# Four-head layer: one matmul for a bound per head, the bias added on GpSimd, normalization and stores inside the loop

## The reference, cut to what matters

```python
x = layernorm(y)                                  # input of the layer, per node over 128 features
Q, K, V = (einsum('bnd,hde->bhne', x, W) for W in (Wq, Wk, Wv))
scores = einsum('bhne,bhme->bhnm', Q, K) / sqrt(32)
scores = where(adj > 0, scores, -inf)
heads = einsum('bhnm,bhme->bhne', softmax(scores, -1), V)
out = concat(heads) @ Wo.T + bo                   # bo: 128 values
y = out + x
result = layernorm(y)
```

## Time and profile before

| | us |
|---|---|
| median of three runs | 1037.8 |
| profiled execution, device time | 1042.1 |
| its span | 1038.0 |
| four-head layer, first to last nb | 674.6 to 981.0 |
| last normalization phase, first operation | 996.1 |
| final check, first operation | 1032.9 |

### The profile page before, as it was taken

How to read it: one execution, slowest core, us unless ns; L and a number is a source line. 1 busy time by engine, 2 the same in 40 slices (tenths; PEclk the granted TensorE clock), 3 DMA queues, 4 the chain that set the end, 5 groups by cost and what they waited for, 6 DMA issues and landing times. The chain is left out here.

```text
span 1038.0 us, 27673 instructions
## 1 busy us (share of the span) xinstructions
PE 783.3 (75%) x9034; PEld 546.0 (53%) x9066; DVE 723.8 (70%) x1912; ACT 508.3 (49%) x1102; POOL 394.5 (38%) x615
## 2 busy tenths in 40 slices
PE   2888888888883777773767776599999999999800
PEld 1555655565652566662555554356665666666500
DVE  2278878888884788895688877455656656556487
ACT  0444444444443888872565666255444554444410
POOL 1455555555641244432555555222222222223100
PEclk9989989999997999996999999699999999999955
DMA  4123333332311122220122222101101011011034
GB/s 118 37 52 77 76 76 76 76 76 76 76 33 21 22 32 30 31 30 11 21 30 26 25 25 25 16 11 17 16 10 15 10 15 15 10 15 16 2 139 185
DMA packets 34627, 43.42 MB, mean 42 GB/s; under 512 B 4361, under 2 KB 22290, under 8 KB 34578
## 3 DMA queue, kind: packets, MB, share of 16 engines
q0 software_dynamic: 18576, 16.82, 12.6%
q1 hardware_dynamic: 16002, 25.97, 8.0%
HBM read 51.19 MB, written 8.39 MB: 57 GB/s over the span
## 5 line engine op out<-in xcount | busy, mean ns | idle before, releaser
L405 DVE SCALAR_TENSOR_TENSOR pp<-banks,floor,adj 128x1024 f32<-128x1024 f32 x128 | 162.1, 1270 | 1.2 <-PE banks L496 1.2
L1081 ACT ACTIVATE pp<-banks,nb 128x512 f32<-128x512 f32 x128 | 81.4, 695 | 85.1 <-issue 59.6
L1049 POOL TENSOR_TENSOR q<-qt 128x512 bf16<-128x512 f32 x32 | 33.0, 1030 | 234.0 <-ACT qt L1074 234.0
L603 DVE TENSOR_SCALAR x<-yres,mean,rstd 128x128 f32 (+1 forms) x256 | 96.6, 439 | 1.8 <-PEq L1752 1.5
L496 PE MATMUL banks<-rows 32*128 32x128 bf16 x1024 | 59.1, 223 | 40.0 <-DVE pp L405 37.4
L509 PE MATMUL banks<-pp,yv 128*17 128x128 f32 x2048 | 84.7, 285 | 1.4 <-DVE pp L405 1.3
L343 ACT COPY rows<-banks 128x640 bf16<-128x640 bf16 x64 | 44.3, 692 | 65.3 <-PE banks L486 65.2
L975 PE MATMUL banks<-w,xt 128*128 128x256 f32 x256 | 73.3, 386 | 0.0
L640 POOL TENSOR_TENSOR yres<-oo,x 128x512 f32 (+1 forms) x32 | 40.3, 1259 | 85.2 <-DVE oo L745 85.2
L348 ACT COPY ot<-banks 128x512 f32<-128x512 f32 x64 | 37.5, 585 | 67.0 <-PE banks L509 66.9
L275 POOL TENSOR_TENSOR yv<-wh,yv 128x512 f32<-128x512 f32 x32 | 35.2, 1099 | 88.3 <-ACT yv L336 88.3
(11 more groups left out here) (198 smaller groups left out, 2151.9 us busy)
## 6 DMA issues: line engine op xcount, KB each, us to landing
adj<-in_adjt POOLq DMA_DIRECT2D x96, 128.0 KB, 3.0
xt<-in_xt SPq DMA_DIRECT2D x32, 256.0 KB, 3.6
x<-in_x SPq DMA_DIRECT2D x32, 256.0 KB, 3.0
out_ngd<-xo SPq DMA_DIRECT2D x32, 256.0 KB, 2.0
adj<-in_adj POOLq DMA_DIRECT2D x32, 128.0 KB, 3.0
ident<-in_ident SPq DMA_DIRECT2D x1, 64.0 KB, 1.9
w<-in_w SPq DMA_DIRECT2D x1, 64.0 KB, 1.8
w0t<-in_w0t SPq DMA_DIRECT2D x1, 64.0 KB, 2.2
```

Source lines behind the costliest of these rows:

```text
L405: nc.vector.scalar_tensor_tensor(pp[:, g], S[g % 2][:, :].rearrange("p (h n) -> p h n", n=N), floor[:, slot:slot + 1], adj[:, slot, g:g + ...
L603: ins = nc.vector.tensor_scalar(xr[:, slot, g, :], yres[:, bass.ds(at, 1), :].rearrange("p o d -> p (o d)"), mean[:, bass.ds(at, 1)], rstd ...
L1081: nc.scalar.activation(pp[:, slot % 2, h], S[h][:, :], ACT.Exp, bias=nb[:, slot % 2:slot % 2 + 1], scale=SCALE).then_inc(s["p"], 1)
```

## The change

It does these things in heads and around it:
- One value bounded the scores of all heads. Now there is one per head: fm, the column maximum, is broadcast as the stationary operand and multiplied by pick (4 columns), which gives the four bounds on all partitions in one matmul. bound_row, bound_max and f1 go. nb has four columns, and negate is a copy. least and rise scale the denominators in place of the constant 2^40.
- The bias matmul in project goes. GpSimd adds bo (a new constant of 128 x 128) to the residual, in biased(t), behind squares(t + 1), and finish reads xb.
- VectorE makes mean and variance of each batch (moments(t - 1), five small operations behind the bn_stats), ScalarE the reciprocal deviation (roots(t - 1), two small activations behind reciprocals(t)), and VectorE normalizes yres in place (result(t - 2), four tensor_scalar ahead of normalize(t + 3)). SyncE stores each batch from yres.
- row_statistics(3) and write_out go.

```diff
@@ -61,6 +61,7 @@
+    k["bo"] = sb("bo_all", [N, D], F32)
@@ -87,7 +88,7 @@
-                 (k["w3v"], c["wv"]), (k["w3ot"], c["wot"]), (a0c, c["a0"]), (hb, c["hb"]), (a1c, c["a1"])]
+                 (k["w3v"], c["wv"]), (k["w3ot"], c["wot"]), (k["bo"], c["bo_all"]), (a0c, c["a0"]), (hb, c["hb"]), (a1c, c["a1"])]
@@ -999,14 +1000,14 @@
-def heads(nc, sb, sem, pb, k, yres, stats, mean, rstd, rsum, adjt):
+def heads(nc, sb, sem, pb, k, yres, stats, mean, rstd, rsum, adjt, out_ngd):
...
-    LN40 = 40.0 * math.log(2.0)
+    HALF = 0.505 * SCALE
@@ -1015,7 +1016,10 @@
-    shift = sb("shift3", [N, 1], F32)
+    pick = sb("pick3", [N, H], F32)
+    least = sb("least3", [N, 2], F32)
+    rise = sb("rise3", [N, 2], F32)
+    xb = sb("xb3", [N, 2, NG, D], F32)
@@ -1023,18 +1027,32 @@
-    f1 = sb("f13", [1, 2], F32)
-    frow = WF[0:1, 0:N]
-    fall = WF[:, 256:257]
-    nb = sb("nb3", [N, 2], F32)
+    fall = WF[:, 256:256 + H]
+    nb = sb("nb3", [N, 2, H], F32)
+    both = sb("both3", [N, 2, NG, 2], F32)
+    apart = sb("apart3", [N, 2, NG], F32)
+    var = sb("var3", [N, 2, NG], F32)
+    inv = sb("inv3", [N, 2, NG], F32)
+    eps = sb("eps3", [N, 1], F32)
+    out_done = sem("l3_out_done")
...
-    s = {n: sem(f"l3_{n}") for n in ("set ln xt_tr xt q qt kk kt v va q2 k2 f fm frow f1 fall nb nota s p o den log rec on "
+    s = {n: sem(f"l3_{n}") for n in ("set ln xt_tr xt q qt kk kt v va q2 k2 f fm fall nb least rise nota xb link sq half var lvar root out s p o den log rec on "
...
+        @block.sync
+        def _(sp):
+            def store(n):
+                sp.wait_ge(s["out"], n + 1)
+                sp.dma_start(out_ngd[:, bass.ds(n * NG, NG), :], yres[:, bass.ds(n * NG, NG), :]).then_inc(out_done, 16)
...
+            with sp.Fori(0, T) as n:
+                store(n)
+            sp.wait_ge(out_done, 16 * T)
...
         def _(pool):
             def load_adj(n, slot):
@@ -1048,6 +1066,12 @@
+            def biased(n, slot):
+                need(pool, s["ln"], n + 1)
+                need(pool, s["y_out"], n - 1)
+                nc.gpsimd.tensor_tensor(xb[:, slot % 2], xr[:, slot], k["bo"][:, :].rearrange("p (o d) -> p o d", o=1).to_broadcast([N, NG, D]),
+                                        ALU.add).then_inc(s["xb"], 1)
@@ -1057,6 +1081,7 @@
+                biased(t, slot)
@@ -1078,17 +1103,32 @@
-                nc.scalar.activation(pp[:, slot % 2, h], S[h][:, :], ACT.Exp, bias=nb[:, slot % 2:slot % 2 + 1],
+                nc.scalar.activation(pp[:, slot % 2, h], S[h][:, :], ACT.Exp, bias=nb[:, slot % 2, h:h + 1],
...
+            def rises(n, slot):
+                need(act, s["least"], n + 1)
+                nc.scalar.activation(rise[:, slot % 2:slot % 2 + 1], least[:, slot % 2:slot % 2 + 1], ACT.Exp).then_inc(s["rise"], 1)
...
             def reciprocals(n, slot):
...
-                nc.scalar.activation(lden[:, :], KD[:, :], ACT.Ln, scale=2.0 ** 40).then_inc(s["log"], 1)
+                need(act, s["rise"], n + 1)
+                nc.scalar.activation(lden[:, :], KD[:, :], ACT.Ln, scale=rise[:, slot % 2:slot % 2 + 1]).then_inc(s["log"], 1)
...
-                nc.scalar.activation(rec[:, slot % 2, :], lden[:, :], ACT.Exp, scale=-1.0, bias=shift[:, :],
+                nc.scalar.activation(rec[:, slot % 2, :], lden[:, :], ACT.Exp, scale=-1.0, bias=least[:, slot % 2:slot % 2 + 1],
...
+            def roots(n, slot):
...
+                need(act, s["var"], n + 1)
+                need(act, s["root"], n)
+                nc.scalar.activation(var[:, slot % 2], var[:, slot % 2], ACT.Ln, bias=eps[:, :], scale=1.0 / D).then_inc(s["lvar"], 1)
+                need(act, s["lvar"], n + 1)
+                need(act, s["out"], n - 1)
+                nc.scalar.activation(inv[:, slot % 2], var[:, slot % 2], ACT.Exp, scale=-0.5).then_inc(s["root"], 1)
@@ -1105,9 +1145,13 @@
+                rises(t, slot)
...
+                if not known(t) or t >= 1:
+                    roots(t - 1, (slot - 1) % RING)
...
+            roots(T - 1, (T - 1) % RING)
...
         def _(dve):
@@ -1133,19 +1177,19 @@
             def bound(n, slot):
...
-                need(dve, s["frow"], n - 1)
+                need(dve, s["fall"], n - 1)
...
-            def bound_max(n, slot):
-                need(dve, s["frow"], n + 1)
-                need(dve, s["fall"], n - 1)
-                nc.vector.reduce_max(f1[0:1, slot % 2:slot % 2 + 1], frow, AX_X).then_inc(s["f1"], 1)
+                need(dve, s["fm"], n + 1)
+                need(dve, s["rec"], n - 1)
+                nc.vector.tensor_scalar(least[:, slot % 2:slot % 2 + 1], fm[:, slot % 2:slot % 2 + 1], HALF, 39.0, ALU.mult, ALU.min).then_inc(s["least"], 1)
             def negate(n, slot):
...
-                nc.vector.tensor_scalar(nb[:, slot % 2:slot % 2 + 1], fall, -SCALE, None, ALU.mult).then_inc(s["nb"], 1)
+                nc.vector.tensor_copy(nb[:, slot % 2, :], fall).then_inc(s["nb"], 1)
             def divide(n, slot):
@@ -1155,20 +1199,45 @@
             def finish(n, slot):
...
+                need(dve, s["xb"], n + 1)
...
-                                        xr[:, slot, :, :], ALU.add).then_inc(s["y_out"], 1)
+                                        xb[:, slot % 2], ALU.add).then_inc(s["y_out"], 1)
             def statistics(n, slot):
...
-                    nc.vector.bn_stats(stats[:, bass.ds(at, 1), :].rearrange("p o d -> p (o d)"),
-                                       yres[:, bass.ds(at, 1), :].rearrange("p o d -> p (o d)"))
+                    ins = nc.vector.bn_stats(stats[:, bass.ds(at, 1), :].rearrange("p o d -> p (o d)"),
+                                             yres[:, bass.ds(at, 1), :].rearrange("p o d -> p (o d)"))
+                ins.then_inc(s["link"], 1)
...
+            def moments(n, slot):
...
+                need(dve, s["link"], 3 * n + 1)
+                st = stats[:, bass.ds(n * NG, NG), :]
+                a, b, v = both[:, slot % 2], apart[:, slot % 2], var[:, slot % 2]
+                nc.vector.tensor_tensor(b, st[:, :, 1], st[:, :, 4], ALU.subtract).then_inc(s["link"], 1)
+                nc.vector.tensor_tensor(a, st[:, :, 1:3], st[:, :, 4:6], ALU.add).then_inc(s["link"], 1)
+                need(dve, s["link"], 3 * n + 3)
+                need(dve, s["root"], n - 1)
+                nc.vector.scalar_tensor_tensor(b, b, D / 4.0, b, ALU.mult, ALU.mult).then_inc(s["sq"], 1)
+                nc.vector.tensor_scalar(a[:, :, 0], a[:, :, 0], 0.5, None, ALU.mult).then_inc(s["half"], 1)
+                need(dve, s["sq"], n + 1)
+                nc.vector.tensor_tensor(v, a[:, :, 1], b, ALU.add).then_inc(s["var"], 1)
...
+            def result(n, slot):
+                need(dve, s["root"], n + 1)
+                need(dve, s["half"], n + 1)
+                for g in range(NG):
+                    y = yres[:, bass.ds(n * NG + g, 1), :].rearrange("p o d -> p (o d)")
+                    ins = nc.vector.tensor_scalar(y, y, both[:, slot % 2, g, 0:1], inv[:, slot % 2, g:g + 1], ALU.subtract, ALU.mult)
+                ins.then_inc(s["out"], 1)
...
-            nc.vector.memset(shift[:, :], LN40)
+            nc.vector.tensor_scalar(pick[:, :], k["headsum"][:, 0:N:E], -HALF / E, None, ALU.mult)
+            nc.vector.memset(eps[:, :], EPS)
@@ -1183,7 +1252,6 @@
-                bound_max(t, slot)
@@ -1194,6 +1262,9 @@
+                    moments(t - 1, c0)
+                if not known(t) or t >= 2:
+                    result(t - 2, (slot - 2) % RING)
@@ -1201,6 +1272,9 @@
+            moments(T - 1, (T - 1) % RING)
+            result(T - 2, (T - 2) % RING)
+            result(T - 1, (T - 1) % RING)
...
         def _(pe):
@@ -1235,13 +1309,10 @@
-            def bound_row(n, slot):
+            def bound_all(n, slot):
...
-                nc.tensor.matmul(frow, fm[:, slot % 2:slot % 2 + 1], k["ident"][:, :], start=True, stop=True).then_inc(s["frow"], 1)
...
-            def bound_all(n, slot):
-                need(pe, s["f1"], n + 1)
-                nc.tensor.matmul(fall, k["onesf"][0:1, :], f1[0:1, slot % 2:slot % 2 + 1], start=True, stop=True).then_inc(s["fall"], 1)
+                nc.tensor.matmul(fall, fm[:, slot % 2:slot % 2 + 1].to_broadcast([N, N]), pick[:, :], start=True, stop=True).then_inc(s["fall"], 1)
             def scores(n, slot):
@@ -1278,12 +1349,9 @@
             def project(n, slot):
...
-                nc.tensor.matmul(WF[:, :], k["ones96"][:, :],
-                                 k["bias3"][:, :].rearrange("p (o d) -> p o d", o=1).to_broadcast([96, NG, D]),
-                                 start=True, stop=False, skip_group_check=True)
...
-                                           start=False, stop=(g == NG - 1), skip_group_check=True)
+                                           start=True, stop=True)
@@ -1300,10 +1368,9 @@
-                bound_row(t, slot)
+                bound_all(t, slot)
...
-                bound_all(t, slot)
@@ -1317,31 +1384,6 @@
```

(27 more changed lines are left out.)

## The result

The changed kernel takes 1049.76 us (median of seven runs), the kernel before 1038.19 beside it. One of the seven took 2462.94 us, a disturbed run that the ratio leaves out; the other six lie from 1043.9 to 1050.21. The ratio of the compared runs is 1.008 with a 95% interval of 1.0057 to 1.0103 (the medians alone would give 1.011): **slower by 0.8%**, where 1032.9 had been forecast. The profiled execution took 1050.21 us, 8.1 more than that of before.

The account below looks back on a forecast made before the run. TensorE was taken to bound the kernel before, VectorE the changed step. Tail -36.2, setup +0.5 and steps +30.8 gave -4.9 us, so 1032.9 from a median of 1037.8; the forecast's own range was 1028 to 1037, the whole range 1020 to 1048.

Parts of the forecast that it names:

- The tail: After the loop: last bn_stats to the check takes 6.67 us, not 42.62; with the last projection's bias matmul, 36.2 saved.
- The setup and the first gaps: Ahead of the loop: one more constant load costs 0.5 us; the first two gaps, without result, put at nothing.
- Who closes the step: In each step: VectorE is late, TensorE idles some 1.7 us ahead of the broadcast matmul; 11.05 us against 9.91.
- The hold: On VectorE beside GpSimd's addition: small operations of moments are held until 0.2 us before the addition ends, at 6.78.
- Rivals 1 and 2: VectorE beside the addition: first, moments not held, step 10.78, 1026 us, chance 0.20; second, nothing held, 9.99, 1004, 0.07.
- Which operation is held: In moments on VectorE: two small operations pass before the addition starts at 5.72; the third waits until 6.78.
- rival 3: Moments on VectorE come too late and stand wholly behind the addition: step 11.25, 1038 us, chance 0.14.
- The eight small waits: Further waits on VectorE without a row, 0 to 0.11 us each: taken at 0.03, together 0.23 a step.
- Rival 4: The eight waits on VectorE lie open at 0.11 each, 0.88 together: step 11.70, 1050 us, chance 0.18.
- The clock: TensorE, idle about 1.7 us a step, might lose its clock: no price, 0.03 left for the clock or a queue.
- The slower side of the range: Whole kernel over 1043 us: open waits on VectorE and some rest, chance 0.20; range up to 1048.
- The base: Whole kernel: profiled 1042.1 us would become 1037.2; the same difference from the median of 1037.8 gives 1032.9.

Follow-up runs that it names:

- experiment 3: The changed kernel with GpSimd's bias addition made twice in a row, the first into a spare tile: 1087.64 us, ratio 1.046 to the kernel before.
- experiment 1: The changed kernel with GpSimd's bias addition moved ahead of the squares, to the step's start: 1007.81 us, ratio 0.9695 to the kernel before.
- experiment 5: The changed kernel with the transposes of t + 2 ahead of the bound's matmul and made twice: 1047.3 us, ratio 1.0072 to the kernel before.
- experiment 4: The changed kernel with the transposes of t + 2 ahead of the bound's matmul and made three times: 1045.75 us, ratio 1.0074 to the kernel before.
- experiment 10: The kernel before with only moments, roots and result in the loop and stores from SyncE: 1023.54 us, ratio 0.9838.
- bias addition alone: The kernel before with only the bias added by GpSimd behind the square of k, no bias matmul: 1038.92 us, ratio 0.9981.

## Why the prediction was wrong

The change of the profiled execution was forecast at -4.9 us and came out at +8.1. Step by step:

- **The tail** was right: 6.67 forecast, 6.93 measured from the last bn_stats to the check. The two small activations are covered (inv ends at 1035.29, while VectorE makes the results until 1036.77).
- **The setup and the first gaps** were right within their size: 0.5 forecast; the last constant that the setup waits for is loaded 0.4 later. What lies between doesn't carry it on: the first nb of the layer stands 0.5 earlier than in the earlier trace rows, within the spread of a few us that executions have ahead of the layer.
- **Who closes the step** was right. TensorE waits 1.57 us for VectorE's column maximum (about 1.7 forecast).
- **The hold** was right, for a class of operation no row of before showed. The held operation's record ends at 733.13 + 1.26 = 734.39; less the 0.17 that it takes alone, it was let go at 734.22, 0.14 before GpSimd's record ends (734.36); 0.2 was taken. Rivals 1 and 2, in which they aren't held, fall: the first would have been 1026 and the second 1004. The Trainium skill, page "SBUF — State Buffer", section "Who interferes with whom", has a VectorE instruction with two SBUF inputs contend with a GpSimd one that reads SBUF: the rows of this kernel agree, down to four elements a partition (1.26 us against 0.17), and so does experiment 3.
- **Which operation is held**: the forecast let two pass and held the third. That is what the undisturbed written-out steps do, and five steps of the loop. In eleven the first is held, as rival 3 has it, since one wait costs 0.18 idle in the loop against 0.03 in the steps written out. It starts at 5.73 after nb, where 5.52 was forecast and the addition starts at 5.71: the two modes are 0.02 us apart. In the step shown result starts at 7.38 after nb in place of 7.05. Steps of either mode in the loop take 11.1 to 11.2 us, so little hung on it.
- **The eight small waits**, at 0.23 together, were mostly too dear: outside of moments VectorE's chain shows none, and from the maximum's start to nb it takes 1.71, forecast 1.72. Rival 4, which had the kernel slower by these waits, didn't occur. This error and the one before it cancel: an undisturbed step takes 11.07 to 11.21, forecast 11.05.
- **The clock is the step that failed.** Under "What else moves" the prediction said that TensorE might lose its clock with 1.7 us idle a step, and waved it away: the third layer has it busy 67% at 0.95. It did lose it: 8.9 us in nine long steps and 2.6 in the tail, where the way from the last nb to the last bn_stats takes 11.63 us at 0.58, and 9.02 at 0.98 in experiment 1. Without these the profiled execution would have been at about -3.4, near the -4.9 forecast. The slower side of the range was built on another mechanism, and the clock had no price in it, only a share of the 0.03 left over.

The sentence failed in its reading of a row, before any question of the chip. The 0.95 of the earlier trace rows is a mean over 450 to 640 us. It comes from the passage between two layers, before 500; in the layer's own steps the clock is at its full level. Two windows of the kernel before:

```profile
470.00:495.00 25.00, 8.25 (x34) 5.88 (x32) 12.72 (x46) 5.71 (x9) 4.91 (x5) 0.59 0.08 11
520.00:640.00 120.00, 86.39 (x678) 65.41 (x679) 96.69 (x244) 73.11 (x146) 68.86 (x73) 1.00 0.23 27
```

So the mean said neither that the third layer keeps its clock nor that it loses a little; and a layer with short waits (1.47 us in each step of 5.06) was no model for one with a long step. Even read rightly, the row wouldn't have given the answer: at 72% busy this layer keeps 1.00, and the changed kernel at 82% doesn't. Busy share alone doesn't tell. What was missing was a rival with a price: a group of projection matmuls takes 1.05, so two such groups at half the rate are at most 2.1 us more for a fall. Half of that in a third of the 27 steps is 9 us, in each of them 28. With that the slower case would have reached past 1050. This is an estimate made afterwards: what share of the steps falls, no row of before gave. (Measured: TensorE took 754.31 - 749.95 = 4.36 for what the next step does in 764.64 - 761.95 = 2.69, and the step was 1.0 longer, 0.7 being taken up by the shorter hold.)

- **The base.** The profiled execution of before lies 3.9 us above the median of its runs, that of after 0.5. The forecast took the difference over to the median as it stood. By medians the miss is 16.5 us: 13.0 in the profiled executions (11.5 the clock, 1.4 the size of steps, the rest small and of both signs: -1.0 ahead of the first nb, +0.95 outside the stretch from it to the check) and 3.5 from the base.

**What stays open** is what exactly lets the clock fall. TensorE waits twice a step. In the kernel after the mean waits are 1.5 (34.6 us in 23 waits, 1.9 the longest) and 0.3, with falls in a third of the steps; 1.0 and 0.57 in experiment 5 go with seven falls; 1.18 and 0.44 in experiment 4 with none; 0.7 and 0.3 in experiment 1 with none, but 0.7 and 0.4 in experiment 10 with one; and the third layer waits for a larger part of its time and has none. The runs fix the cause (TensorE's idle time in this loop) and the price, not the rule.

## What to carry to other kernels

- When work goes to GpSimd, ask what VectorE does in the same microsecond. Here a small operation on VectorE with two inputs from SBUF became as long as the GpSimd operation it fell beside; the same addition cost some 40 us more behind the square of k than where VectorE waits for TensorE, and there under 3.
- When an edit makes another engine close the loop, TensorE begins to wait, and its clock is a cost of its own: read it in the stages and in the single steps, put a price on one fall, and make it a rival. A stage's mean is no model until it has been split.
- Parts that pay alone may lose together, once the engine that covered their cost is no longer the last. Find out who closes the step after each part, and place new work in the waits of the engine that closes it: with nothing but placement and written-out steps the same arithmetic took 972.7 us and not 1049.8.

## What the runs showed of the hardware

- An operation of VectorE on 128 x 4 elements takes up to 1.28 us in place of 0.17 beside one addition on GpSimd (kernel after, L1219); four normalizations take 2.11 in place of 1.11 (bias addition alone). bn_stats beside a square of GpSimd keeps 0.86, and the copies from TensorE's banks keep 0.69.
- Between two additions of GpSimd in a row at most one more small operation of VectorE gets through, and the next stands for most of the second one (it takes 1.12 to 1.31 us, add_twice).
- More work on TensorE can make a kernel faster: twelve spare transposes a step brought the ratio from 1.008 to 1.0022 (medians 1049.8 and 1040.9), with the granted clock at 1.00 in place of 0.95 from 700 to 960 us.
- A step of the loop costs 9.19 to 9.6 us where the same step written out costs 8.81. A register's value for a wait takes 93 ns in the trace (FUSED_REGOPS ahead of L1219, 24 times), and the wait of L1219 then shows 0.18 us idle, put down to VectorE's own result, where the written-out one shows 0.03. That the registers are what a loop step loses is the likely reading; the runs change the loop as a whole.
